# Attention scores of two token tiles in one pass, both attend products one tile later

## What is computed

```python
h = _layernorm(x) * (1 + ca) + sa
q = (hs @ q_w.T + q_b).reshape(B, L, nh, d)      # hs = h, nh = 16, d = 128
k = (hs @ k_w.T + k_b).reshape(B, L, nh, d)
v = (hs @ v_w.T + v_b).reshape(B, L, nh, d)
beta = jax.nn.softplus(hs @ b_w.T + b_b)
qn, kn, gv = _l2norm(q / scale), _l2norm(k / scale), beta[..., None] * v
# chunks of c = 64 tokens
attn = jnp.einsum('bnhid,bnhjd->bnhij', qc, kc)
mask = jnp.where(causal, decay, 0.0)             # decay is 1 where causal
out = jnp.einsum('bnhij,bnhjd->bnhid', attn * mask, gvc)
out = (out * jax.nn.silu(hs @ og_w.T)) @ o_w.T + o_b
x = x + ga * out
x = x + gb * moe(_layernorm(x) * (1 + cb) + sb)
```

## Time and profile before

| what | us |
|---|---|
| median of three runs (2166.52 to 2167.47) | 2167.18 |
| the profiled execution, whole | 2164.84 |
| its span from first to last instruction | 2163.1 |
| PE busy in the span | 2135.4 |
| DVE busy | 1154.5 |
| ACT busy | 1031.5 |
| POOL busy | 522.2 |

### The profile page before, as it was taken

The page is one execution under the profiler, slowest core; times in us unless marked ns, Lnnn a source line. Parts: engine busy times, 40 slices in busy tenths (PEclk is TensorE's granted clock), DMA queues, the critical chain, the costliest instruction groups (busy, mean ns, idle before and its releaser), DMA issues.

```text
span 2163.1 us, 36173 instructions
## 1 busy us (share of the span) xinstructions
PE 2135.4 (99%) x12463; PEld 1752.6 (81%) x12463; DVE 1154.5 (53%) x2174; ACT 1031.5 (48%) x3300; POOL 522.2 (24%) x540
## 2 busy tenths in 40 slices
PE   8999999999999999999999999999999999999999
PEld 6778888888888887878888888888888888888887
DVE  6555654555555555555554445555555455545554
ACT  6655664665665665565565453333332333333232
POOL 2433443443443343343343441000000000000000
PEclk9999999999999999999999999999999999999999
DMA  8574443254355354354233221342334234323221
GB/s 264 185 239 133 146 138 123 81 162 139 93 145 159 84 154 136 95 147 142 106 143 113 70 107 49 129 170 98 127 125 149 88 121 156 103 97 113 96 94 63
DMA packets 191892, 274.79 MB, mean 127 GB/s; under 512 B 99184, under 2 KB 132960, under 8 KB 191712
## 3 DMA queue, kind: packets, MB, share of 16 engines
q1 hardware_dynamic: 191712, 272.49, 39.6%
HBM read 214.79 MB, written 57.67 MB: 126 GB/s over the span
## 4 chain that ended last, share of the span: by engine, by line
PE 92%; DVE 3%; ACT 2%; issue 2%; DMA 1%; DVEq 0%; POOL 0%; SPq 0%; ACTq 0%; POOLq 0%
PE proj_ps L651 49%; PE out_ps L651 14%; PE av_ps L877 5%; PE s_ps L866 4%; PE s_ps L924 3%; PE av_ps L924 3%; PE qt_ps L924 3%; PE kt_ps L924 3%; PE qt_ps L847 2%; PE kt_ps L852 2%; DMA head_scr<-stage 1%; PE misc_ps L670 1%; PE out_ps L721 0%; ACT squares L1117 0%; PE misc_ps L679 0%
## 5 line engine op out<-in xcount | busy, mean ns | idle before, releaser
L651 PE MATMUL proj_ps<-w_qkv,h_t 128*128 128x512 f32 x2304 | 618.0, 406 | 10.3 <-DVE q_sb L1428 2.1
L651 PEld LDWEIGHTS proj_ps<-w_qkv,h_t 128*128 128x128 f32 x2304 | 407.9, 188 | 103.3 <-issue 20.2
L651 PE MATMUL proj_ps<-h_t,w_qkv 128*128 128x512 f32 x1800 | 444.2, 391 | 0.3 <-issue 0.2
L651 PEld LDWEIGHTS proj_ps<-h_t,w_qkv 128*128 128x128 f32 x1800 | 335.6, 188 | 70.2 <-issue 1.3
L608 POOL TENSOR_TENSOR inv_norm<-guarded,minus_half 128x8 f32<-128x8 f32 x128 | 209.4, 1636 | 741.9 <-DVE guarded L1441 741.9
L1108 ACT ACTIVATE q_t<-qt_ps 128x512 f32<-128x512 f32 x128 | 76.3, 596 | 303.9 <-PE qt_ps L847 303.4
L651 PE MATMUL proj_ps<-h_t,w_gate 128*128 128x512 f32 x768 | 190.2, 398 | 2.6 <-ACT gate L1131 1.3
L1428 DVE TENSOR_TENSOR v_sb<-proj_ps,bias 128x512 f32<-128x512 f32 x128 | 88.5, 691 | 190.0 <-PE av_ps L877 183.4
L1117 ACT ACTIVATE squares<-q_sb 128x128 f32<-128x128 f32 x512 | 151.4, 297 | 56.9 <-DVE q_sb L1428 52.4
L1428 DVE TENSOR_TENSOR q_sb<-proj_ps,bias 128x512 f32<-128x512 f32 x128 | 88.4, 690 | 165.5 <-PE proj_ps L651 160.7
L651 PEld LDWEIGHTS proj_ps<-h_t,w_gate 128*128 128x128 f32 x768 | 139.8, 188 | 40.2 <-ACT gate L1131 10.7
(11 more groups left out here) (216 smaller groups left out, 3174.5 us busy)
## 6 DMA issues: line engine op xcount, KB each, us to landing
w_qkv<-tile_scr SPq DMA_DIRECT2D x100, 768.0 KB, 4.3
w_qkv<-head_scr SPq DMA_DIRECT2D x45, 1024.0 KB, 11.0
head_scr<-stage SPq DMA_DIRECT2D x30, 512.0 KB, 3.8
w_gate<-head_scr SPq DMA_DIRECT2D x15, 1024.0 KB, 4.9
w_out<-head_scr SPq DMA_DIRECT2D x15, 1024.0 KB, 4.9
tile_scr<-stage SPq DMA_DIRECT2D x25, 512.0 KB, 3.1
x_in<-_attn_hidden_states_dram SPq DMA_DIRECT2D x16, 512.0 KB, 6.7
h_scr<-stage SPq DMA_DIRECT2D x16, 512.0 KB, 3.3
```

The source lines that it names most:

```text
L651: mm = pe.matmul(out, w, y, start=(j == 0 and m == 0), stop=(3 * j + m == n - 1))
```

## The change

score takes two units: score(m) makes units 2m+1 and 2m+2 at odd n from 3 on, 16 matmuls instead of 8, and lays them side by side in the one bank: 64 columns for each head, 4 heads, two units, in the upper 64 partitions the second chunks. Nothing is computed for the off-diagonal halves. mask is two DVE operations, each 64 partitions x 8 x 64, which write into the diagonal halves of an array scores of twice the size; the rest of it is cleared once at the start by POOL. q_t and k_t get two halves, one for each unit of the pair. Both attends stand in the next unit, at even n from 4 on: attend(n-3) between K and V, attend(n-2) behind V. v_sb gets four buffers, and its add waits for attended n-3.

What depends on it moves. The gates of a block go from t = 1 to t = 2, the output projection and its adds from t = 2 to t = 3, the low parts to two at t = 1 and two at t = 2. Both side chains start a unit later. SP's loads of output and gate weights go one unit later. Space is made elsewhere: V's bias has one buffer (`bias[:, 4]`), which load_v_bias fills at a group's first unit, after the last V add of the group before; Q's and K's biases keep two. The squares of Q and K share one buffer, and delta shares xn's.

```diff
-            n = 32 * q - 1 + 8 * a
+            n = 32 * q + 8 * a
...
-            n = 32 * q + 15 + 8 * a
+            n = 32 * q + 16 + 8 * a
...
-    free = lambda n, p: (n % TS, p) != (1, 1) and not any(t[0] in CHUNKS + p * ("prob", "exp", "log", "norm") or t[:2] == ("split", "f") for t in side[n, p])
+    free = lambda n, p: (n % TS, p) != (2, 1) and not any(t[0] in CHUNKS + p * ("prob", "exp", "log", "norm") or t[:2] == ("split", "f") for t in side[n, p])
...
-        causal = sb("causal", [P, P])
+        causal = sb("causal", [P, CH])
...
-        bias = sb("bias", [P, 2, 3, HG * P])
-        raw = [[sb(f"{n}_sb{b}", [P, HG * P]) for b in range(2)] for n in "qkv"]
-        squares = sb("squares", [P, 2, HG * P])
+        bias = sb("bias", [P, 5, HG * P])
+        raw = [[sb(f"{n}_sb{b}", [P, HG * P]) for b in range(4 if n == "v" else 2)] for n in "qkv"]
...
-        scores = sb("scores", [P, HG * P])
+        q_t, k_t = sb("q_t", [P, 2, HG * P]), sb("k_t", [P, 2, HG * P])
+        scores = sb("scores", [P, 2, HG, P])
...
-                for j, src in enumerate((q_b, k_b, v_b)):
-                    sp.dma_start(bias[:, gi % 2, j, :],
+                for j, src in enumerate((q_b, k_b)):
+                    sp.dma_start(bias[:, 2 * (gi % 2) + j, :],
                                  src[(gi % NG) * 512:(gi % NG + 1) * 512].rearrange("(a n) -> a n", a=1)
                                  .partition_broadcast(P).rearrange("p a n -> p (a n)")).then_inc(bias_loaded[gi % 2], 16)
+            def load_v_bias(gi):
+                after(sp, biased[V], 8 * gi)
+                sp.dma_start(bias[:, 4, :], v_b[(gi % NG) * 512:(gi % NG + 1) * 512].rearrange("(a n) -> a n", a=1)
+                             .partition_broadcast(P).rearrange("p a n -> p (a n)")).then_inc(v_bias_loaded, 16)
...
+                if r == 0 and gi:
+                    load_v_bias(gi)
...
-            ORDER = [(w, t) for t in range(2) for w in (Q, K, V)] + [("gate", h) for h in range(HG)] + \
-                    [(w, t) for t in range(2, TS) for w in (Q, K, V)]
+            pe.wait_ge(made, 4)
+            ORDER = [(w, t) for t in range(3) for w in (Q, K, V)] + [("gate", h) for h in range(HG)] + \
+                    [(w, 3) for w in (Q, K, V)]
...
-            def score(n):
-                pe.wait_ge(qt_copied, n)
-                pe.wait_ge(kt_copied, n)
-                after(pe, masked, n - 1)
-                if n == 1:
+            def score(m):
+                pe.wait_ge(qt_copied, 2 * m + 2)
+                pe.wait_ge(kt_copied, 2 * m + 2)
+                after(pe, masked, m)
+                if m == 0:
                     pe.wait_ge(gained, 3)
-                for h in range(HG):
-                    for c in range(P // CH):
-                        at = slice(h * P + c * CH, h * P + (c + 1) * CH)
-                        mm = pe.matmul(s_ps[c * CH:(c + 1) * CH, at], k_t[:, at], q_t[:, at], start=True, stop=True)
+                for j in range(2):
+                    for h in range(HG):
+                        for c in range(P // CH):
+                            at = slice(h * P + c * CH, h * P + (c + 1) * CH)
+                            mm = pe.matmul(s_ps[c * CH:(c + 1) * CH, (j * HG + h) * CH:(j * HG + h + 1) * CH],
+                                           k_t[:, j, at], q_t[:, j, at], start=True, stop=True)
                 mm.then_inc(scored, 1)
             def attend(n):
-                pe.wait_ge(masked, n)
+                pe.wait_ge(masked, (n + 1) // 2)
                 pe.wait_ge(v_scaled, n)
                 after(pe, gated_done, n - 1)
                 if n == 1:
                     pe.wait_ge(boot_lo, 10)
                 for h in range(HG):
                     at = slice(h * P, (h + 1) * P)
-                    mm = pe.matmul(av_ps[:, at], raw[V][(n - 1) % 2][:, at], scores[:, at], start=True, stop=True)
+                    mm = pe.matmul(av_ps[:, at], raw[V][(n - 1) % TS][:, at], scores[:, (n - 1) % 2, h, :],
+                                   start=True, stop=True)
                 mm.then_inc(attended, 1)
...
-            for n in range(N + 2):
+            for n in range(N):
                 i, t = divmod(n, TS)
-                if n < N:
-                    project(i, t, Q)
-                    for task in side[n, 0]:
-                        do(task)
-                    project(i, t, K)
-                if t == 2 and i:
+                project(i, t, Q)
+                for task in side[n, 0]:
+                    do(task)
+                project(i, t, K)
+                if t == 3 and i:
                     project_out(i - 1, 0)
-                if n >= N:
-                    up(n - N, 0)
-                if n >= 2:
-                    score(n - 1)
-                if n == N:
-                    up(0, 1)
-                if n == N + 1:
-                    down(0)
-                if n < N:
-                    project(i, t, V)
-                if t == 2 and i:
+                if n % 2 and n >= 3:
+                    score(n // 2 - 1)
+                if n % 2 == 0 and n >= 4:
+                    attend(n - 3)
+                project(i, t, V)
+                if t == 3 and i:
                     project_out(i - 1, 1)
-                if n >= 2:
-                    attend(n - 1)
-                if 1 <= n <= N:
+                if n % 2 == 0 and n >= 4:
+                    attend(n - 2)
+                if n:
                     turn(n)
                 if n < 2:
                     boot_chunk((G, O)[n], 0)
...
                     boot_chunk((G, O)[n], 1)
                 if n == 1:
                     mod_turn(1, s_ps[:, 2 * P:4 * P], 2)
-                if n < N:
-                    for task in side[n, 1]:
-                        do(task)
-                if t == 1 and n < N:
+                for task in side[n, 1]:
+                    do(task)
+                if t == 2:
                     for h in range(HG):
                         project_gate(i, h)
...
             def add_bias(n, what):
                 i, t = divmod(n, TS)
                 if what == Q and n % 8 == 0:
-                    dve.wait_ge(bias_loaded[(n // 8) % 2], 48 * (n // 16 + 1))
+                    dve.wait_ge(bias_loaded[(n // 8) % 2], 32 * (n // 16 + 1))
+                if what == V and n % 8 == 0:
+                    dve.wait_ge(v_bias_loaded, 16 * (n // 8 + 1))
                 dve.wait_ge(projected[what], n + 1)
-                after(dve, (q_turned, k_turned, attended)[what], n - 1)
+                after(dve, (q_turned, k_turned, attended)[what], n - 3 if what == V else n - 1)
                 at = (t + what) % 2
-                dve.tensor_tensor(raw[what][t % 2][:, :], proj_ps[at][:, :], bias[:, (i // 2) % 2, what, :], ALU.add)\
+                dve.tensor_tensor(raw[what][t if what == V else t % 2][:, :], proj_ps[at][:, :], bias[:, 4 if what == V else 2 * ((i // 2) % 2) + what, :], ALU.add)\
                    .then_inc(biased[what], 1)
-            def mask(n):
-                dve.wait_ge(scored, n)
-                after(dve, attended, n - 1)
-                dve.tensor_tensor(heads(scores[:, :]), heads(s_ps[:, :]),
-                                  causal[:, :].unsqueeze(1).broadcast_to([P, HG, P]), ALU.mult).then_inc(masked, 1)
+            def mask(m):
+                dve.wait_ge(scored, m + 1)
+                after(dve, attended, 2 * m)
+                for c in range(P // CH):
+                    at = slice(c * CH, (c + 1) * CH)
+                    i = dve.tensor_tensor(scores[at, :, :, at].rearrange("p a h n -> p (a h) n"),
+                                          s_ps[at, :].rearrange("p (a n) -> p a n", n=CH),
+                                          causal[at, :].unsqueeze(1).broadcast_to([CH, 2 * HG, CH]), ALU.mult)
+                i.then_inc(masked, 1)
...
-            for n in range(N + 2):
+            for n in range(N):
                 i, t = divmod(n, TS)
-                if n < N:
-                    add_bias(n, Q)
-                    add_bias(n, K)
+                add_bias(n, Q)
+                add_bias(n, K)
+                if t == 3 and i:
+                    add_out(i - 1, 0)
+                if n % 2 == 0 and n >= 4:
+                    apply_gate(n - 3)
+                if n % 2 and n >= 3:
+                    mask(n // 2 - 1)
+                if t == 1 and i:
+                    lo_part(n - 4)
+                    lo_part(n - 3)
+                for task in side[n, 0]:
+                    do(task)
+                add_bias(n, V)
+                sum_squares(n)
+                if t == 3 and i:
+                    add_out(i - 1, 1)
+                if n % 2 == 0 and n >= 4:
+                    apply_gate(n - 2)
                 if t == 2 and i:
-                    add_out(i - 1, 0)
-                if n == N + 1:
-                    lo_hidden(0)
-                if n >= 2:
-                    mask(n - 1)
```

(2 more changed lines are left out.)

197 lines of the change are left out of this document (114 added, 83 removed).

## The result

| | median us | against before, 95% interval |
|---|---|---|
| before | 2166.52 (2164.82 to 2167.47) | |
| changed | 2174.15 (2172.59 to 2177.88) | 1.0039 [1.0026, 1.0051] |

A forecast was written before the change was run, and what follows sets the result against it. PE was taken to bound the kernel, busy 2135.4 of 2163.1 us. Terms from -22.4 for score visits to +9.7 for the norm summed to +4.4: 2169.2 profiled, 2171.5 by the median, forecast 2167 to 2176, range 2155 to 2181.

The forecast's parts named there:

- the start: Boot: without gate steps before the first turn of xn, PE idles 6.0 in place of .34; +5.2 us (2 to 6).
- V's bias: Group boundaries: single-buffered bias load late behind SP's store and weight loads, at n = 8, 24, 40, 48; +6.2 us (0 to 15).
- the clock: Slow granted clock on PE behind the hole at the start; +2.5 us.
- the norm: Next supertile's layer norm at t=1 comes late behind DVE's masks and low parts; PE waits 1.62 at six supertiles, +9.7 us.
- statistics: Six x1-part units, t=1: DVE's statistics delay the next Q's add, V's projection waits .57 each; +3.4 us (0 to 6).
- gates: Gates at t=2: their banks hang on ACT, busy with side chains; an estimate, +1.0 us (-1 to 3).
- Score visits: PE's score: 64 visits of 1.29 us replace 128, each saving .35 for entering and leaving; -22.4 us.
- Rival D: Score: the change doesn't save per visit, 32 records cost two times .82; sum +27, 2194 us; chance .03.
- Attend visits: PE: 64 more attend visits, alone between K and V at even units, cost nothing net; 0, bound +6 us.
- rival C: An attend between two projections costs .09 each: +6, 2177 us; chance .20 together with Rival B.
- Rival A: DVE's chain at t=1 costs PE nothing: 2158 us, or 2152 with V's bias hidden as well; chance .22.
- Rival B: V's bias is late at most boundaries: +8 to +14, 2180 us; chance .20 together with rival C.

The follow-up runs named there:

- n5_split: The changed kernel with each pair's score cut in two visits of 16 records, between Q and K and between K and V: 2190.51 us.
- n11_split: The changed kernel with all four repairs (norm and low parts, statistics, V's bias, first gates), each pair's score cut in two visits of 16 records: 2156.02 us.
- n3_vbias: The changed kernel with SP's load of V's bias issued between the two slots of a group's last unit, ahead of its second store and weight loads: 2169.47 us.
- n10_lo: The changed kernel with only the two low parts at t = 1 moved behind V's bias add on DVE: 2159.0 us.

## Why the prediction was right, and where it was off

**The sign, the size and the mechanism.** I forecast 2171.5 us, 4.4 us more by the profile, with .47 for slower. It is 2174.15, within the range of 2155 to 2181, and 7.8 more by the profile. That it is slower hung on the steps at t = 1 and on the start, and all of them are in the trace. The terms were less exact than the sum: V's bias and the clock were 4.2 us too dear, the norm, statistics, gates and the phase's end 7.9 too cheap. That these errors partly cancelled is luck, and with it part of the nearness of the sum. The profiled execution, moreover, has the low clock at the start alone; where it falls at unit 25 too, about one us comes on top that no term of the prediction had.

**Score visits.** Right: 1.29 us for a visit of 32 records was predicted, 1.28 to 1.29 measured. Rival D is out (n5_split, n11_split). What I hadn't seen is that the .35 depends on the neighbours: .28 before transposes, .11 before other narrow matmuls.

**Attend visits.** Right at 0; rival C (6 us) is out by the starts at 806.44, 807.24 and 808.70.

**The norm.** Right in mechanism, 1.6 forecast and 1.9 measured. I let the score end 1.29 behind K and the mask start there; the mask starts 1.20 behind the score's start, the chain from there is 4.00 where I had 3.79, PE is ready 3.45 behind where I had 3.54, and the turn starts .15 after xn's end. That masks on 64 partitions cost as much as on 128, which rows 9 had to stand for, is right: .69 each. Rival A (DVE's chain costs nothing) is out.

**The statistics.** Right in place, 3.4 for 5.4 in size. The count to Q's add came to 8.7 behind K's end with every operation at its mean; in the trace V's projection waits for it by .67 to .95 where I had .57. The count left out the gap of .21 that DVE shows between each stage copy or x_in sum and the add behind it, twice in this chain.

**V's bias.** The over-sized term: late boundaries were forecast at units 8, 24, 40 and 48, 6.2 us; the bias was late at 8, 24, 40 and 64, and PE waited at one, 2.7. The step that failed is that I put the lateness of V's add on PE in full. PE needs that bank only when K of the next unit is projected, which is some 2 us after. Rival B is out: n3_vbias gains nothing elsewhere. That the clock can fall behind such a wait was counted for the start and not here.

**Gates and side tasks.** Under-sized, 1.0 against 4.4. I had no row for it and took ACT for the cause. For one wait that is right: the gate at unit 10 waits 1.73 for ACT, behind a store, and that wait stays with the low parts moved (in n10_lo it stands at unit 14). For the rest n10_lo points to DVE's low parts: 7.3 us in the units with gates go with them, 5 of these at the gates' steps. That is more than the change added, for a part was in the kernel before, in which every unit has one low part ahead of V's add. How the 4.4 divide between the two is open.

```profile
14.80 0.60 PE L778 MATMUL qt_ps<-ident,gate 128*128 128x128 f32 x4
```

For the price I took the whole slow stretch of the boot, and here about 3.2 us of work stood in it. The table's 1.8 is what remains of the start's 6.9 and holds .4 of something else.

## What to carry to other kernels

On an engine with an in-order queue that sets the time, count visits to another mode as well as instructions, and then look at every engine that feeds it for what the move queues up ahead of the operand it needs next. The changed kernel was 8 us slower as it stood and 26 us faster once two orders on DVE, a slot of the plan, a place in SP's queue and 24 matmuls at the start had been put right. Moving two operations that nobody waits for behind one that somebody waits for took their whole time (1.2 us) out of each of the six waits, but such a move pays only where nothing urgent stands right behind.
